# First partial sum of a selective scan moved from VectorE to an accumulating DMA of GpSimd, with a seventh state buffer and a new placement of the side jobs

## What is computed

```python
u, gate = split(h @ W_in.T)                   # 1024 -> 2 x 2048 channels
u = silu(conv4(u) + conv_b)                   # 4 taps along time
dt, Bm, Cm = rmsnorm(split(u @ Wx.T))         # 64, 16, 16
delta = softplus(dt @ Wdt.T + dt_bias)
# for every channel d and each of 16 states n, along time:
state = exp(delta * A) * state + delta * u * Bm
y = sum_n(state * Cm)                         # 16 products to be summed
x = x + ((y + u * D) * silu(gate)) @ W_out.T
x = x + experts(base2(x))                     # softmax, top 2 of 8
```

## Time and profile before

| | |
|---|---|
| median of 3 runs | 2556.78 us (2555.78 to 2558.4) |
| the profiled execution | 2555.34 us, span 2553.6 us |
| mean granted TensorE clock | 0.945 of full speed |
| first scan of slot 0, first scan of slot 127 | 135.9 us, 2476.3 us from the span's start |

### The profile page before, as it was taken

One profiled execution on the slowest core, in us unless ns is written; L12 is line 12 of the kernel. 1 busy time (PEld: TensorE's weight loads), 2 busy tenths in 40 slices (PEclk: granted clock), 3 DMA queues, 4 the chain that ended last, 5 costly groups with the idle time before them and its releaser, 6 DMA issues.

```text
span 2553.6 us, 30492 instructions
## 1 busy us (share of the span) xinstructions
PE 2273.3 (89%) x10128; PEld 1918.1 (75%) x10128; DVE 2234.1 (87%) x2098; ACT 1620.3 (63%) x3768; POOL 2121.3 (83%) x1092
## 2 busy tenths in 40 slices
PE   7978898899879997999889997899978978787878
PEld 6867786688768886788768886788867766666767
DVE  1369797899989998999989998999989999999892
ACT  1367566776577766775667665776667765776550
POOL 0088787899889998999979998999979998999880
PEclk9989999899899998999999998999989998888989
DMA  6363443444345433544445433544426332432332
GB/s 209 125 212 100 115 142 119 151 142 139 119 171 155 140 133 105 197 149 140 125 142 168 148 126 116 177 160 136 135 70 215 116 108 91 169 120 90 116 104 89
DMA packets 132250, 350.05 MB, mean 137 GB/s; under 512 B 38573, under 2 KB 43181, under 8 KB 130621
## 3 DMA queue, kind: packets, MB, share of 16 engines
q1 hardware_dynamic: 109326, 296.19, 36.1%
q10 hardware_dynamic: 22768, 51.93, 6.0%
HBM read 337.04 MB, written 11.02 MB: 136 GB/s over the span
## 4 chain that ended last, share of the span: by engine, by line
PE 51%; DVE 22%; ACT 12%; issue 7%; POOL 7%; ACTq 1%; DMA 0%; SPq 0%; DVEq 0%; POOLq 0%
DVE scan L1241 12%; PE late L666 11%; PE ubank L584 10%; PE ubank L613 9%; ACT scan L1076 7%; DVE st L1253 5%; PE gbank L566 5%; POOL st L1464 3%; POOL st L1472 2%; PE scan L584 2%; PE small L640 2%; DVE ubank L1222 2%; PE gbank L630 2%; PE scan L566 1%; ACT ubank L937 1%
## 5 line engine op out<-in xcount | busy, mean ns | idle before, releaser
L1464 POOL TENSOR_TENSOR st<-w_sb,bc 128x1024 f32<-128x1024 f32 x512 | 1198.1, 2355 | 163.5 <-PE gbank L630 150.2
L1241 DVE TENSOR_TENSOR_SCAN scan<-scan,st 128x1024 f32<-128x1024 f32 x512 | 1156.5, 2285 | 40.1 <-POOL st L1464 22.7
L1076 ACT ACTIVATE scan<-delta,A_sb 128x255 f32<-128x255 f32 x2048 | 846.2, 459 | 0.0
L1472 POOL TENSOR_TENSOR st<-st 128x1024 f32<-128x1024 f32 x256 | 603.1, 2356 | 73.1 <-DVE st L1253 63.0
L584 PE MATMUL ubank<-h,wt 128*128 128x256 f32 x1712 | 445.2, 419 | 130.5 <-ACT qg L1155 125.7
L613 PE MATMUL ubank<-h,wt 128*128 128x256 f32 x2048 | 481.6, 390 | 41.5 <-ACT qg L1155 36.3
L584 PEld LDWEIGHTS ubank<-h,wt 128*128 128x128 f32 x1712 | 360.1, 213 | 208.4 <-ACT qg L1155 150.6
L1073 ACT ACTIVATE scan<-iota 128x4 f32<-128x4 f32 x512 | 86.8, 170 | 655.0 <-DVE st L1253 631.6
L613 PEld LDWEIGHTS ubank<-h,wt 128*128 128x128 f32 x2048 | 400.4, 196 | 103.7 <-ACT qg L1155 40.9
L1253 DVE TENSOR_TENSOR st<-scan,bc 128x1024 f32<-128x1024 f32 x384 | 453.7, 1207 | 0.0
L666 PE MATMUL late<-yg,wt 128*128 128x256 f32 x1792 | 410.5, 388 | 32.6 <-DVE x L1278 29.6
(11 more groups left out here) (217 smaller groups left out, 2253.8 us busy)
## 6 DMA issues: line engine op xcount, KB each, us to landing
wt<-in_W_in SPq DMA_DIRECT2D x256, 512.0 KB, 3.6
wt<-in_W_out SPq DMA_DIRECT2D x128, 512.0 KB, 3.4
wt<-in_cond_W SPq DMA_DIRECT2D x64, 512.0 KB, 3.6
bc<-bc_rows ACTq DMA_DIRECT2D x64, 512.0 KB, 6.6
wt<-G_tiles SPq DMA_DIRECT2D x32, 512.0 KB, 3.6
wt<-in_ffn_B SPq DMA_DIRECT2D x26, 512.0 KB, 3.4
xb<-in_x SPq DMA_DIRECT2D x8, 1024.0 KB, 5.6
x<-in_x ACTq DMA_DIRECT2D x28, 256.0 KB, 3.9
```

The costliest lines, as they stand in the source:

```text
L1076: last = fn(t[:, k, 1:T], delta[:, c, 1:T], ACT.Exp, scale=A_sb[:, col:col + 1])
L1241: v_.tensor_tensor_scan(Tps[q % 2][:, :], Tps[q % 2][:, :], x_, 0.0, ALU.mult, ALU.add).then_inc(scan_done, 1)
L1464: tt(st[:, n % ST_RING, :, :], w_sb[:, i % 2:i % 2 + 1, :].to_broadcast([P, NQ, T]), bc[:, 0, q * NQ:(q + 1) * NQ, :], ALU.mult).then_inc( ...
L1472: tt(st[:, n % ST_RING, :, :], st[:, n % ST_RING, :, :], st[:, (n - 1) % ST_RING, :, :], ALU.add).then_inc(add_done, 1)
```

## The change

VectorE's `add_first` goes. Product 1 is written to its state buffer like the others, and GpSimd issues a DMA that adds product 0's buffer onto product 1's (`add_dma(i, 1)`, 512 KB within SBUF, accumulating), as its first item of slot i; its `add(i, 2)` waits for the landing. The ring of state buffers grows from 6 to 7, with other waits in `dbu`. To make room the constant `sel` goes (`weights_b` uses slices of `ident`, eight products in place of four per batch) and `wT` shares `la`'s memory. The jobs are placed anew: `xp` moves from the end of slot 12 to its small job, in two parts; `A` 1, `cond`, `wb`, `B` and `Bs` move; `g`, `b2` and `bias` of batch 0 move; the loads and stores of `x2` move with them. The diff, cut:

```diff
-ST_RING = 6
+ST_RING = 7
 def u_chunks(i):
     if b == 0:
-        if c <= 5:
+        if c <= 4:
             return [NC + 2 * (c - 1), NC + 2 * c - 1]
-        if c <= 11:
-            return [NC + 10 + (c - 6)]
+        if c <= 10:
+            return [NC + 8 + (c - 5)]
+        if c == 11:
+            return [NC + 14, NC + 15]
 def late_job(i):
     if b == 0:
-        return {13: ("g", 0, 7), 14: ("b2", 0, 0), 15: ("bias", 0, 0)}.get(c)
+        return {13: ("b2", 0, 0), 14: ("g", 0, 5), 15: ("g", 0, 6)}.get(c)
     if c == 0:
-        return ("B", f - 1, 2) if f else None
+        return ("B", f - 1, 1) if f else ("g", 0, 7)
...
-    if c in (10, 11):
-        return ("A", f, c - 10)
-    if c in (12, 13):
-        return ("wb", f, c - 12)
-    return ("B", f, c - 14)
+    if c == 10:
+        return ("A", f, 0)
...
+    if c == 11:
+        return ("cond", j, 6) if j < B else None
+    return {12: ("wb", f, 0), 13: ("A", f, 1), 14: ("wb", f, 1), 15: ("B", f, 0)}[c]
 def small_job(i):
+    if b < LAST and c >= 12:
+        return {12: ("xp", b + 1, 0), 13: ("ms", b + 1, 0), 14: ("dt", b + 1, 1), 15: ("dt", b + 1, 2)}[c]
-        return ("g", 0, c - 6) if c <= 12 else None
+        return ("g", 0, c - 6) if c <= 10 else ("bias", 0, 0)
-    if c in (6, 9) and j < B:
-        return ("cond", j, {6: 3, 9: 6}[c])
+    if c == 9 and j < B:
+        return ("cond", j, 4)
 def half_job(i):
-        return ("la", 3, 0) if f == 0 else ("Bs", f - 1, 7)
-    if j < B and c in (1, 3, 5, 7, 8, 9):
-        return ("cond", j, {1: 0, 3: 1, 5: 2, 7: 4, 8: 5, 9: 7}[c])
+    if f and c <= 2:
+        return ("Bs", f - 1, 5 + c)
+    if f == 0 and c == 1:
+        return ("la", 3, 0)
+    if j < B and c in (3, 5, 7, 8, 9, 11):
+        return ("cond", j, {3: 0, 5: 1, 7: 2, 8: 3, 9: 5, 11: 7}[c])
     if c == 15 and b < LAST:
-        return ("Bs", f, 6)
+        return ("Bs", f, 4)
 def end_job(i):
-        if c == 12:
-            return ("xp", b + 1, 0)
...
 # TensorE, job "g"
-                    if k < KH - 1:
-                        for v in u_chunks(5):
+                    if k < 5:
+                        for v in u_chunks(4):
                             pe.wait_ge(u_done, v + 1)
...
 # TensorE, job "xp" (small) and behind ubank_free(i)
+                    x_proj(job, range(NC - 1 if i % NC == 12 and i >= NC else NC - 2))
...
+                if small_job(i) and small_job(i)[0] == "xp":
+                    x_proj(small_job(i), range(NC - 1 if i >= NC else NC - 2, NC))
 # ScalarE: pro_cond(1, 4..7) of slot 0 one by one between decays of slots 0 and 1
 # VectorE
-                if q == 1:
-                    v_.tensor_tensor(Tps[1][:, :], Tps[1][:, :], cq, ALU.mult).then_inc(prod_done, 1)
-                else:
-                    v_.tensor_tensor(plane(n), Tps[q % 2][:, :], cq, ALU.mult).then_inc(mul_done, 1)
-
-            def add_first(i):
-                dve.wait_ge(prod_done, i + 1)
-                dve.wait_ge(mul_done, 4 * i + 1)
-                v_.tensor_tensor(plane(4 * i + 1), Tps[1][:, :], plane(4 * i), ALU.add).then_inc(mul_done, 1)
+                v_.tensor_tensor(plane(n), Tps[q % 2][:, :], cq, ALU.mult).then_inc(mul_done, 1)
 # GpSimd, dbu(i, q)
-                if q == 2 and i:
-                    pool.wait_ge(mul_done, 4 * i - 2)
-                if q == 1 and i >= 2:
+                if q == 2 and i >= 2:
                     pool.wait_ge(id_mm, i - 1)
+                if q == 3 and i:
+                    pool.wait_ge(acc_st[0], 16 * i)
...
+            def add_dma(i, k):
+                n = 4 * i + k
+                pool.wait_ge(mul_done, n + 1)
...
+                pool.dma_start(st[:, n % ST_RING, :, :], st[:, (n - 1) % ST_RING, :, :], accum_op=ALU.add
+                               ).then_inc(acc_st[k - 1], 16)
             def add(i, k):
-                if k == 3:
+                if k == 2:
+                    pool.wait_ge(acc_st[0], 16 * (i + 1))
+                else:
                     pool.wait_ge(add_done, 3 * i + 1)
 # GpSimd, the slot
+                add_dma(i, 1)
                 for b, j in softplus_of(i - 1):
                     delta_add(b, j)
```

More of the change, by code:

```diff
@@ L134, in end_job @@
     b, c = split(i)
-    if b < LAST:
-        if c == 12:
-            return ("xp", b + 1, 0)
-        if c == 13:
-            return ("dt", b + 1, 0)
-    return None
+    return ("dt", b + 1, 0) if b < LAST and c == 13 else None
 def slot_jobs(i):
@@ L157, in takes_half @@
 def takes_half(i):
-    return late_job(i) if late_job(i) and late_job(i)[0] in ("g", "b2", "bias") else half_job(i)
+    if late_job(i) and late_job(i)[0] in ("g", "b2"):
+        return late_job(i)
+    return small_job(i) if small_job(i) and small_job(i)[0] == "bias" else half_job(i)
 def job_tiles(job):
@@ L214, in build @@
           A_mat, D_par, W_out, base_W, base_b, lora2_A, lora2_B, GT_all, ffn_B,
-          ident_in, mean_in, sel_in, iota_in, out):
+          ident_in, mean_in, iota_in, out):
     with ExitStack() as ctx:
@@ L312, in u_home @@
                 return quarter(v % 4)
-            return late if NC <= v < NC + 10 and v % 2 else ubank
+            return late if NC <= v < 2 * NC and v % 2 and (v < NC + 8 or v == 2 * NC - 1) else ubank
         def cv_home(v):
@@ L362, in build @@
         scan_done = sem("scan_done")
-        prod_done = sem("prod_done")
         mul_done = sem("mul_done")
         add_done = sem("add_done")
+        acc_st = [sem(f"acc_st{i}") for i in range(2)]
         id_mm = sem("id_mm")
@@ L592, in h0_ready @@
                 else:
-                    pe.wait_ge(*emptied(("cond", b, 6)))
-                    pe.wait_ge(*emptied(("cond", b, 7)))
+                    for m in (4, 6, 7):
+                        pe.wait_ge(*emptied(("cond", b, m)))
             def ubank_free(i):
@@ L631, in sum_states, with x_proj @@
                 last.then_inc(id_mm, 1)
-            def x_proj(job):
+            def x_proj(job, cs):
                 b = job[1]
-                pe.wait_ge(u_done, NC * (b + 1))
-                for c in range(NC):
+                pe.wait_ge(u_done, NC * b + cs[-1] + 1)
+                for c in cs:
                     n = TILE_NO[("wx", b, c // 8)]
@@ L641, in x_proj @@
                               start=(c == 0), stop=(c == NC - 1))
-                last.then_inc(done_inc(job), 1)
+                if cs[-1] == NC - 1:
+                    last.then_inc(done_inc(job), 1)
             def mean_square(job):
@@ L721, in weights_b @@
             def weights_b(m, o):
-                return mm(o, sel[:, m * P:(m + 1) * P], wT[:, :], start=True, stop=True)
+                for e in range(2):
+                    pick = ident[0:E, 2 * m + e:2 * m + e + 1].to_broadcast([E, ER])
+                    last = mm(o[e * ER:(e + 1) * ER, :], pick, wT[:, :], start=True, stop=True)
+                return last
             def expert_out(f, m, o):
@@ L791, in run @@
                     else:
-                        pe.wait_ge(half_ev, HALF_NO[("cond", 2, 7)] + 1)
                         pe.wait_ge(yg_done, i - 1)
                     transformed(lambda kk: wt[:, n % W_RING, kk, :], o[:, 0:GX],
-                                late[:, 0:T] if k < KH - 1 else gbank[:, T:2 * T]).then_inc(inc, 1)
+                                late[:, 0:T] if k < 5 else gbank[:, T:2 * T]).then_inc(inc, 1)
                 elif kind == "b2":
                     pe.wait_ge(b2_ld, 16 * B)
+                    pe.wait_ge(*emptied(("bias", 0, 0)))
                     pe.wait_ge(yg_done, i - 1)
@@ L801, in run @@
                 else:
+                    pe.wait_ge(half_ev, HALF_NO[("cond", 2, 7)] + 1)
                     pe.wait_ge(yg_done, i - 1)
@@ L1030, in evac @@
                     act.wait_ge(*made(job))
+                    if b + 3 < B:
+                        act.wait_ge(*made(("cond", b + 3, 7)))
                     fn(wT[:, :], o[0:E, 0:T], ACT.Copy).then_inc(ev_inc(job), 1)
@@ L1124, in _ @@
                         softplus(n, j)
-                if i == NC:
+                    if i == 1:
+                        pro_cond(1, 6)
+                if i == NC + 1:
                     for k in range(PAIRS):
                         load_x2(0, k)
+                if b >= 2 and c in (1, 2, 4):
+                    for k in {1: [0], 2: [1, 2], 4: [3]}[c]:
+                        load_x2(b - 1, k)
                 if c == 15 and b < LAST:
@@ L1397, in _ @@
                     soft_max_step(b - 1, 3)
-                add_first(i)
                 if weigh:
@@ L1499, in _ @@
                 fold(i)
-                if i + 1 < CHUNKS:
+                if not last:
                     dbu(i + 1, 3)
```

84 lines of the change are left out of this document (42 added, 42 removed).

## The result

The changed kernel takes 2531.85 us in the median (2530.05 to 2533.04), the kernel before 2556.28 (2551.16 to 2558.4) on the same chip: ratio 0.9907, 95% interval 0.989 to 0.9924. Predicted were 2505 us, 51 less; measured are 24 less. The direction was right and 2531.85 lies in the range, but the gain is a little under half of what was forecast.

The account below looks back on a forecast made before the run. It took a loop of TensorE, ScalarE and VectorE at 17.6 us a slot as the bound, GpSimd in batch 7. 2555.3 - 75.8 (placement) + 9 + 15 (issues) = 2503.5, hence 2505 us; range 2475 to 2600.

Parts of the forecast that it names:

- the first one under *The placement: Slots 13 and 14, batches 0 to 5: `xp` run earlier removes the stall, 6.5 plus 2.0 a batch, 51 us gained.
- the stall moves: Slot 13: `A` 1 ahead of `ms` delays `norm`, ScalarE stands in `ms_evac`, half of 51 us stay, 2530; chance 0.13.
- Slot 11: Batches 0 to 5: without `add_first` VectorE needs 17.2 us, hence the loop's 17.6; 1.2 x 6 = 7.2 us gained.
- the first slots of batches 0 and 1: Rest of batch 0's excess and batch 1's first slot, with less to catch up: 8 us gained, an estimate.
- slot 6 of batch 0: With `g` 0 waiting for chunks of slot 4, the slot falls to its 43 products, 18.6 us: 11.1 gained.
- `Bs`: Slots 2 and 3: four `Bs` put 0.4 us more on VectorE in each, 0.8 x 6 = 5 us lost.
- The issue: DMA issue on GpSimd's queue, 1.0 us each: 9 us lost where GpSimd is late at times, 15 where it bounds.
- Batches 6, 7 and the tail: Issues count whole where GpSimd bounds, 15 us, and `weights_b` costs 1 us in the tail: 16 us lost.
- slot 8: TensorE's slots 1 to 8 hold fewer products, so slot 8 falls to 17.6 us: 0.9 x 5 = 4.5 gained.
- the dear issue: Rival: GpSimd becomes the bound everywhere, decisive from 1.65 us an issue; 2598 us at 2.0; chance 0.17.
- the late landing: Rival: past 7.8 us each further us costs GpSimd up to 1 us a slot; 9 us give 2555; chance 0.10.
- `add_first` that counts in the slots with taps: Rival: if taps didn't wait for ScalarE, GpSimd would set the pace, 2490 us, 2475 with cheap issue; chance 0.08.

Follow-up runs that it names:

- the fastest version: Changed kernel with u copies ahead of `decay(i, 2)`, `ms` ahead of `A` 1, `wT` behind the cond product, VectorE's addition in all slots, no DMA: 2459.97 us.
- the plain copy: Changed kernel with a plain copy in place of the accumulating DMA, result lacking product 1 of each chunk: 2524.62 us in one execution.

## Why the prediction was half right

**The step that failed** is the first one under *The placement*: `A` 1 ahead of `ms` makes the mean square come "about when VectorE reaches `norm`", hence 6 x 8.5 = 51 us. For VectorE that was nearly so: it waits 1.10 us. The order was seen, but its price was looked for at VectorE alone and set to nothing. The engine that pays is ScalarE, which stands for `ms` 3.95 us in its program with a decay and the silu behind it, and from there the delay goes to TensorE's u chunk, the `dt` product and the taps. It could have been worked out: `A` 1 alone is 18 products, 7.8 us. Measured are 16.1 us in place of 51. The order of two jobs, with all else kept, brings back the 35.8 that are missing, and slots 13 and 14 then stand at 18.5 and 17.3 where 18.3 and 17.3 were forecast. So `xp`'s part was sized rightly, as its way back (6.8 us a batch) shows too, and `ms` ate it. The rival "the stall moves" named this mechanism with a chance of 0.13 and half of the gain; it took more than two thirds, and its time of 2530 came within 2 us by luck of the other terms.

**Slot 11**: forecast -7.2, measured +5.0. The term took VectorE's busy time of 17.2 without `add_first` for hidden in a loop of 17.6, and left out two things. The softmax's last step can't be hidden (0.7 a slot), so that even with nothing else changed the addition was worth 0.4 us there and not 1.2. And a `cond` block now stands behind `wT`, which waits for the softmax, with `y_sum` behind that (with `wT` moved, 6.4 us come back). The count was off too: batch 0 has no softmax in slot 11, which lasts 17.2 before and after.

A third thing costs up to 0.7 us, in single batches. In the window of slot 11 above VectorE is busy for 18.56, though 1.22 went, as one small instruction took 1.29 us in place of 0.15; in batches 1, 2, 3 and 5 of that kernel it took 0.30, 0.30, 0.23 and 0.80. Timeline of VectorE and of POOL, slot 11 of batch 4, kernel after, and VectorE of the kernel before:

```profile
1507.92 1.29 DVE L1337 CAST tixf<-tix 128x16 f32<-128x16 uint32 x1
```

```profile
1504.37 4.81 POOL L1492 TENSOR_TENSOR st<-st 128x1024 f32<-128x1024 f32 x2
```

```profile
1541.16 0.15 DVE L1328 CAST tixf<-tix 128x16 f32<-128x16 uint32 x1
```

The cast ends at 1509.21, as GpSimd's two `add` do at 1509.18; the casts of batches 1 to 6 of this kernel all end within 0.03 us after a GpSimd instruction. In the kernel before it began just between two GpSimd instructions, one recorded until 1541.11 and one from 1541.18. In the fastest version it takes 1.92 us in batch 4 and ends with a `dbu` (1472.88 and 1472.84), and slot 11 is full with VectorE:

```profile
1464.90:1485.50 20.60, 18.98 (x90) 16.17 (x89) 20.18 (x31) 11.22 (x28) 17.25 (x9) 1.00 0.51 154
```

What it costs is seen where it differs from batch to batch. With the DMA alone it took 1.44, 0.16, 1.19, 0.29 and 1.04 us in batches 1 to 5, and slot 11 lasted 19.13, 18.40, 18.88, 18.39 and 18.74: the slot grows by what the cast takes above some 0.7 us. That the cast waits for GpSimd's instruction is read from coincidences of this kind; no run was made to move it. The Trainium skill (SBUF — State Buffer, SBUF: two separate sides) says that VectorE and GpSimd share a port pair as an exclusive lock, which the one that starts first holds for its whole instruction, and that certain VectorE instructions need that pair. The rows agree with such a lock; that this cast is one of those instructions is shown by them alone.

**Mis-sized, with the mechanism right**: the first slots of batches 0 and 1 gave 15.3 (8 predicted, an estimate and called one; by its own words, half of 10.9 and a like sum, it would be 10.9); slot 6 of batch 0 fell to 17.3 (18.6 predicted), gaining 12.4; `Bs` cost 2.6 (5, over one batch more). The issue costs 0.84 to 0.93 us (1.0), and the slots in which GpSimd is late lost 5.8 (9). Batches 6, 7 and the tail lost 10.7 (16), but not as the sum had it: batch 7's first nine slots lost 13.3 where nine issues were forecast, 9 us, and its last six gained 4.4, a gain that the sum didn't have: with the jobs placed alike, these six are 5.4 us shorter with the DMA than with `add_first`.

**Right**: slot 8 (-5.0, predicted -4.5), and 17.6 a slot with the placement alone, too. The addition by itself is worth nothing where the taps wait for ScalarE (wait 1.58, predicted 1.53); without any price it is worth 7 us in the whole kernel. The landing takes 6.1 us (6) and is nearly hidden: 15 waits, 21.3 us of GpSimd's time in all. With the DMA and the old placement the kernel is 0.3% slower; what the DMA loses it loses mostly by its issue where GpSimd is the bound. Of the rivals, the dear issue (from 1.65 us), the late landing (from 7.8 us) and `add_first` that counts in the slots with taps are each excluded by those numbers.

The formula of the Trainium skill (DMA: Bandwidth & Descriptors, Anatomy of one DMA) gives an estimate of 3.2 us for 512 KB: the plain copy took 3.2. The Trainium skill (Collectives: The Full Stack, The bandwidth ceiling) says of the reduce-scatter that it runs at half the rate of a copy, as its add reads two sources; the doubled share of the queue here, 13.9% against 6.7%, agrees. The prediction's estimate of 4.4 us from the two pages is what the fastest landing took (4.4); the median one took 6.1 and the slowest 11.4.

What stays open: batch 7's first slots lost more than their issues; two waits for the landing there (1.37 and 0.84 us) are part of that, the rest was not followed up; the placement alone was not taken apart further in batch 0 and in batch 1's first slot, where 15.3 us came from more than one move. And why the early copy of u makes batch 0 longer (296.5 against 289.1 us) was not followed up.
